# Turning the normalised rows with DMA transposes instead of TensorE transposes

## The chip, the cores and the metric

The kernel runs on one core of a Trainium2 chip. A core has TensorE (matrix products into PSUM), VectorE, ScalarE and GpSimd (element-wise work), and SyncE, whose queue issues the DMAs here; 16 DMA engines carry them. The metric is the device time of one execution in microseconds (us), lower is better.

## The reference

The input is x, 4096 rows (2 x 2048) of 1024 columns in fp32. For each row on its own:

```python
n = layernorm(x)
q, k, v = n @ wq.T + bq, n @ wk.T + bk, n @ wv.T + bv      # 1024 -> 1024, seen as 32 heads x 32
s = softmax(einsum("hd,td->ht", q, k) / sqrt(32))           # heads of one row attend to each other
x = x + einsum("ht,td->hd", s, v)
m = layernorm(x)
top2 gate of m @ gate_w.T (8 experts), softmax of the two
x = x + m @ base_w.T + base_b + 2 * sum over experts of gate * (m @ A_e.T) @ B_e.T   # rank 16
```

Attention goes over the 32 heads of one row, so no row needs another one.

## The kernel before, in words

It is written with explicit engine programs and semaphores. The rows are worked through in T = 32 tiles of 128 rows, one row a partition. Each engine has its own program of the same shape (`pipeline`): `step(0)`, a loop over t = 1 to 30 of `step(t, prev=True, nxt=True)`, `step(31, prev=True, nxt=False)`, and `tail(32)`. In step t the attention of tile t goes on beside the end of tile t-1 (attention's context, second layernorm, router and LoRA, base product, result) and the preparation of tile t+1 (first layernorm). The order of work on each engine is written out by hand, and an engine runs it strictly in that order.

All products are made with fp16 parts. A normalised row tile `xn` (fp32) is scaled and split into a high part (`x_hi` for the first layernorm, `x2_hi` for the second, an fp16 cast) and a low part (`x_lo`, `x2_lo`, what the cast left out). A product takes the parts in three combinations, or in two while the weights' low parts are zero, as they are for q, k and v here. TensorE needs the rows turned, with the 1024 columns on the partitions in 8 chunks of 128.

The steps that the change touches, by their order in a loop step t:

- TensorE: `project` runs k, q and v as two halves of 512 columns each. k half 1 and q half 0 have the context products of tile t-1 threaded between them (`attend_one`). After v half 0 comes `turn_rows(t-1)`: eight fp32 transposes of `xn` into PSUM (`turn_ps`). After v half 1 comes `experts(t-1)`: 24 products of 136 columns with router and LoRA weights, from `x2_hi` and `x2_lo`. Then `turn_rows(t+1)`, then `dense(0, k_parts)`: half of the base product, with the attention scores of tile t threaded in (semaphore `scored`), then `turn_low`, `dense(1)`, `dense_lora`.
- ScalarE: `rows_hi` casts each half of `turn_ps` to the high part. Tile t-1's comes after the high part of k, tile t+1's after the first quadrant copy of q (`spread_quadrant`), and behind that is the cast of the turned v (L568).
- VectorE: `normalise` writes `xn` (one buffer for both layernorms). `rows_lo` subtracts the high part from `turn_ps`, in two halves (L684). Tile t-1's comes after the first v bias, tile t+1's after `gating`; behind that VectorE waits for `scored` and takes the scores' maximum (L887).
- SyncE's queue: in each step the load of x tile t+1 into `ld`, the load of x tile t again as residual into `res`, and the store of tile t-1, each behind a wait for the buffer it uses.

At the start the weights of q, k, v, the small matrix `ag` (router and LoRA, rows of 544 bytes) and the base matrix are loaded, their maximum sums are taken on ScalarE (`sums`), and they are split into parts.

In the trace, tiles carved from one large buffer (`ld`, `xn`, `ev`, `turned`, `parts`, `k_parts`, `diag`, `soft`, `res`, `x1`, `y`) are all called work, and x2_hi and x2_lo appear as x_hi and x_lo.

Of the kernel before, what the change touches and what calls it, by code (L numbers as in the profile page):

```python
# [27 lines left out]
P = 128  # L28
# [34 lines left out]
def block_kernel(nc, x, wT, agT, lora_b, biases, out):  # L63
    T = x.shape[0] // P
    with ExitStack() as ctx:
# [117 lines left out]
        den = sb("den", [P, QD])  # L183
        inv = sb("inv", [P, QD])
# [15 lines left out]
        turn_ps = ps("turn_ps", [P, HID])  # L200
# [39 lines left out]
        xt_done = sem("xt_done")  # L240
# [38 lines left out]
        x2t_done = sem("x2t_done")  # L279
# [49 lines left out]
        def _(sp):  # L329
            sp.dma_start(ld, rows(x, 0)).then_inc(ld_loaded, 16)  # L330

            def load(g):
# [11 lines left out]
            load("k")  # L344
            load("q")
# [8 lines left out]

            sp.wait_ge(w_lo_done, n_split)
            sp.dma_start(res, rows(x, 0)).then_inc(res_loaded, 16)
# [17 lines left out]
            pipeline(sp, step, lambda t: store(t - 1))  # L374
# [86 lines left out]
        def _(act):  # L461
# [30 lines left out]
            def rows_hi(t, dst, done, ready):  # L492
                for h in range(2):

                    act.wait_ge(done, 2 * t + h + 1)
                    c = KC // 2
                    nc.scalar.copy(dst[:, h * c:(h + 1) * c, :],  # L497
                                   turn_ps[:, h * HALF:(h + 1) * HALF].rearrange("p (k n) -> p k n", k=c)
                                   ).then_inc(ready, 1)

            rows_hi(0, x_hi, xt_done, xhi_ready)
# [34 lines left out]
            def low_copy(p):  # L536
# [3 lines left out]
                nc.scalar.copy(low_t[:, :], low_ps[:, 0:P]).then_inc(lowt_ready, 1)  # L540

            def step(t, prev, nxt):
                if prev:
# [4 lines left out]
                    rows_hi(t - 1, x2_hi, x2t_done, x2hi_ready)  # L548
# [39 lines left out]
            def tail(t):  # L588
                rows_hi(t - 1, x2_hi, x2t_done, x2hi_ready)
# [7 lines left out]
        def _(dve):  # L597
# [81 lines left out]
            def rows_lo(t, dst, hi, hi_ready, ready):  # L679
                c = KC // 2  # L680
                for h in range(2):

                    dve.wait_ge(hi_ready, 2 * t + h + 1)
                    nc.vector.tensor_tensor(dst[:, h * c:(h + 1) * c, :],  # L684
                                            turn_ps[:, h * HALF:(h + 1) * HALF].rearrange("p (k n) -> p k n", k=c),
                                            hi[:, h * c:(h + 1) * c, :], ALU.subtract).then_inc(ready, 1)
# [46 lines left out]
            rows_lo(0, x_lo, x_hi, xhi_ready, xlo_ready)  # L733
# [70 lines left out]
            def norm2(p):  # L804

                dve.wait_ge(xt_done, 2 * p + 2)
# [21 lines left out]
            def step(t, prev, nxt):  # L828
# [9 lines left out]
                if prev:  # L838
                    norm2(t - 1)
# [4 lines left out]
                if prev:  # L844
# [3 lines left out]
                    rows_lo(t - 1, x2_lo, x2_hi, x2hi_ready, x2lo_ready)  # L848
                    if nxt:

                        dve.wait_ge(x2t_done, 2 * t)
# [74 lines left out]
            def tail(t):  # L926
                attention_end(t - 1)
                ln_stats(1, x1, mv2)
                norm2(t - 1)
                rows_lo(t - 1, x2_lo, x2_hi, x2hi_ready, x2lo_ready)  # L930
# [13 lines left out]

# [224 lines left out]
```

## Time and profile before

| | |
|---|---|
| median of 3 runs | 1545.02 us (1543.29 to 1545.65) |
| span of the profiled execution, first to last instruction | 1543.5 us |
| mean granted TensorE clock | 0.986 |
| TensorE products busy | 1367.9 us, 89% |
| VectorE busy | 1261.1 us, 82% |
| ScalarE busy | 503.8 us, 33% |
| GpSimd busy | 210.7 us, 14% |
| DMA moved | 70.52 MB, 46 GB/s over the span |

The profile was taken by the hardware on one execution. It has a span but no separate time of its own, so its 1543.5 us stand beside the runs: the median is 1.5 us above it. The time of a product is modelled and overlaps its neighbour's, so TensorE's 89% is not a share of its peak. "Idle before, released by" is the time that an engine stood before an instruction and what ended it. A granted clock of 1.00 is 2.4 GHz, 0.50 is 1.2 GHz.

### The profile page before, as it was taken

The page shows a single profiled execution, that of the slowest core. Times are in us where ns is not written, and L with a number is a line of the kernel's source. Part 1 is how long each engine was busy: PE and PEld are TensorE (multiplying, and loading weights), DVE is VectorE, ACT ScalarE, POOL GpSimd, SP SyncE. Part 2 cuts the span into 40 slices and gives each one's busy share as a digit, 9 for nine tenths or more (in the row PEclk, how much of TensorE's full clock was granted, in tenths as well). Part 3 has the DMA queues.
Part 4 walks back from the last instruction along what each step waited for, and adds up shares of the span by engine and source line. Part 5 has one row for each costly group of instructions (what it writes and reads, how often), then busy time and mean ns, then how long its engine had stood idle before and what let it go on. Part 6 is the DMA issues. An engine that isn't in the chain of part 4 may idle for free.

```text
span 1543.5 us, 30006 instructions
## 1 busy us (share of the span) xinstructions
PE 1367.9 (89%) x12432; PEld 750.4 (49%) x12432; DVE 1261.1 (82%) x1751; ACT 503.8 (33%) x572; POOL 210.7 (14%) x280
## 2 busy tenths in 40 slices
PE   0777999999999999999999999999999999999996
PEld 0444445545544554554455455445545544554553
DVE  5778888888888888888888888888888888888874
ACT  7952222333222233322223332222333222233320
POOL 0011110011111001111100111110011111001110
PEclk9989999999999999999999999999999999999997
DMA  9401111000111100011110101111000111100000
GB/s 380 165 1 42 41 41 37 31 29 25 41 41 41 37 31 29 25 41 41 41 35 33 31 23 41 41 41 36 32 31 24 41 41 41 38 30 30 24 29 28
DMA packets 20208, 70.52 MB, mean 46 GB/s; under 512 B 2144, under 2 KB 3168, under 8 KB 20192
## 3 DMA queue, kind: packets, MB, share of 16 engines
q1 hardware_dynamic: 20192, 70.30, 12.8%
q8 instruction: 11, 0.18, 0.1%
q14 instruction: 5, 0.04, 0.0%
HBM read 53.51 MB, written 16.78 MB: 46 GB/s over the span
## 4 chain that ended last, share of the span: by engine, by line
DVE 61%; PE 14%; issue 10%; ACT 6%; DVEq 5%; DMA 3%; SPq 0%; POOL 0%; ACTq 0%; POOLq 0%
DVE work L308 6%; DVE work L800 6%; DVE x_lo L684 5%; PE acc L965 5%; DVE work L725 5%; PE acc L976 5%; DVE work L872 4%; DVE work L843 4%; DVE work L718 4%; DMA work<-x_dram 3%; DVE work L794 3%; DVE work L889 3%; DVE work L911 3%; DVEq L751 3%; DVE work L906 2%
## 5 line engine op out<-in xcount | busy, mean ns | idle before, releaser
L1018 PE MATMUL acc<-base_parts,x_hi 128*128 128x512 f16 x1024 | 325.0, 381 | 32.4 <-DVE work L308 32.4
L956 PE MATMUL attn_ps<-work 128*128 128x32 f16 x2048 | 329.0, 177 | 2.7 <-DVE work L718 1.7
L957 PE MATMUL attn_ps<-work 128*128 128x32 f16 x2048 | 327.3, 176 | 0.0
L958 PE MATMUL attn_ps<-work 128*128 128x32 f16 x2048 | 326.9, 176 | 0.0
L957 PEld LDWEIGHTS attn_ps<-work 128*128 128x128 f16 x2048 | 189.7, 96 | 201.6
L308 ACT COPY work<-work 32x2048 f16<-32x2048 f16 x96 | 182.1, 1897 | 139.2 <-DVE work L718 88.3
L956 PEld LDWEIGHTS attn_ps<-work 128*128 128x128 f16 x2048 | 193.7, 96 | 6.0 <-issue 3.6
L965 PE MATMUL acc<-w_hi_k,x_hi 128*128 128x512 f16 x512 | 140.6, 385 | 62.1 <-DVE work L718 28.4
L1018 PE MATMUL acc<-base_parts,x_lo 128*128 128x512 f16 x512 | 194.4, 380 | 0.0
L958 PEld LDWEIGHTS attn_ps<-work 128*128 128x128 f16 x2048 | 188.9, 96 | 0.0
L668 DVE BATCH_NORM_STATS2 stats<-work 128x6 f32<-128x512 f32 x128 | 82.3, 685 | 126.4 <-DMA work<-x_dram 125.3
L718 DVE TENSOR_TENSOR work<-work 128x1024 f16<-128x1024 f32 x96 | 117.4, 1223 | 54.7 <-ACT work L568 37.9
L384 POOL TENSOR_TENSOR var<-mv,eps 128x1 f32<-128x1 f32 x64 | 12.1, 190 | 1072.2 <-DVE mv L671 1072.2
L497 ACT CAST x_hi<-turn_ps 128x512 f16<-128x512 f32 x128 | 68.1, 579 | 266.4 <-PE turn_ps L949 266.4
L725 DVE SCALAR_TENSOR_TENSOR work<-acc,acc_to_a,biases_sb 128x512 f32<-128x512 f32 x192 | 138.8, 736 | 12.3 <-PE acc L976 6.4
L1018 PEld LDWEIGHTS acc<-base_parts,x_hi 128*128 128x128 f16 x1024 | 101.2, 99 | 97.5 <-DVE work L308 39.4
L965 PE MATMUL acc<-w_hi_q,x_hi 128*128 128x512 f16 x512 | 138.5, 380 | 10.7 <-DVE work L725 8.4
L526 ACT CAST work<-work 128x1024 f16<-128x1024 f32 x32 | 33.4, 1045 | 336.9 <-DVE work L821 336.9
L976 PE MATMUL acc<-w_hi_k,x_lo 128*128 128x512 f16 x512 | 137.8, 379 | 0.0
L976 PE MATMUL acc<-w_hi_q,x_lo 128*128 128x512 f16 x512 | 137.2, 378 | 0.0
L965 PE MATMUL acc<-v_parts,x_hi 128*128 128x512 f16 x512 | 122.5, 383 | 8.0 <-DVE v_parts L640 8.0
L976 PE MATMUL acc<-v_parts,x_lo 128*128 128x512 f16 x512 | 121.0, 379 | 0.0
(135 smaller groups left out, 2231.4 us busy)
## 6 DMA issues: line engine op xcount, KB each, us to landing
work<-x_dram SPq DMA_DIRECT2D x64, 512.0 KB, 3.5
out_dram<-work SPq DMA_DIRECT2D x32, 512.0 KB, 2.8
work<-wT_dram SPq DMA_DIRECT2D x19, 512.0 KB, 9.5
v_parts<-wT_dram SPq DMA_DIRECT2D x8, 512.0 KB, 14.8
base_parts<-wT_dram SPq DMA_DIRECT2D x5, 512.0 KB, 12.1
biases_sb<-bias_dram SPq DMA_DIRECT2D x4, 512.0 KB, 15.2
work<-agT_dram SPq DMA_DIRECT2D x1, 544.0 KB, 4.7
lora_up<-lora_b_dram SPq DMA_DIRECT2D x1, 512.0 KB, 15.8
```

Source lines behind the costliest of these rows:

```text
L308: copy(diag[s, :, :, s], parts[s, :, :, :]).then_inc(ready, 1)
L668: nc.vector.bn_stats(stats[:, i, h, :], src[:, h * HALF:(h + 1) * HALF])
L684: nc.vector.tensor_tensor(dst[:, h * c:(h + 1) * c, :], turn_ps[:, h * HALF:(h + 1) * HALF].rearrange("p (k n) -> p k n", k=c), hi[:, h * ...
L718: nc.vector.tensor_tensor(parts[:, :, 1, :], turned3, parts[:, :, 0, :], ALU.subtract).then_inc(lo_ready, 1)
L725: nc.vector.scalar_tensor_tensor(out=ev[:, s], in0=acc[bank][:, :], scalar=acc_to_a[:, i:i + 1], in1=bias[g][:, s], op0=ALU.mult, op1=ALU. ...
L800: nc.vector.scalar_tensor_tensor(out=x1, in0=ev, scalar=ctx_undo[:, 0:1], in1=res, op0=ALU.mult, op1=ALU.add).then_inc(x1_ready, 1)
L956: nc.tensor.matmul(dst, diag[:, i, 0, :], moving[:, i, 0, :], start=True, stop=False)
L957: nc.tensor.matmul(dst, diag[:, i, 0, :], moving[:, i, 1, :], start=False, stop=False)
L958: return nc.tensor.matmul(dst, diag[:, i, 1, :], moving[:, i, 0, :], start=False, stop=True)
L965: nc.tensor.matmul(dst, x_hi[:, k, :], w_hi[g][:, k, cols], start=(k == 0), stop=False)
L976: mm = nc.tensor.matmul(dst, x_lo[:, k, :], w_hi[g][:, k, cols], start=False, stop=(k == KC - 1))
L1018: nc.tensor.matmul(dst, rows_part[:, m // 3, :], w_part[:, m // 3, cols], start=(m == 0), stop=False)
```

## The change

The normalised row tile is split before it is turned. ScalarE casts all of `xn` to `row_hi` (fp16), VectorE subtracts it from `xn` into `row_lo`, and SyncE's queue issues one DMA transpose for each part, from `row_hi` to `x_hi` or `x2_hi` and from `row_lo` to `x_lo` or `x2_lo`. TensorE's `turn_rows` and the PSUM tile `turn_ps` are gone. TensorE now waits for the transposes' landings (16 per transpose) before `experts` and before k half 0. ScalarE and VectorE wait, before they write `row_hi` or `row_lo` again, until the transpose that read it has landed. For tile t+1 the transposes are issued after v's last product of step t, since that reads the old `x_hi`. The first residual load moves behind the transposes of tile 1, and SyncE's loop is written out as 30 steps. Some small buffers share storage now.

```diff
+        row_hi = sb("row_hi", [P, HID], F16)
+        row_lo = sb("row_lo", [P, HID], F16)
         low = sb("low", [P, ER])
-        low_t = sb("low_t", [P, P])
-        den = sb("den", [P, QD])
-        inv = sb("inv", [P, QD])
+        den = top
+        inv = top
-        hot1 = sb("hot1", [P, EXPERTS])
-        hot2 = sb("hot2", [P, EXPERTS])
-        w_full = sb("w_full", [P, EXPERTS])
+        hot1 = best
+        hot2 = logits
+        w_full = best_no
-        turn_ps = ps("turn_ps", [P, HID])
...
+            def turn_rows(t, hi, hi_split, hi_ready, lo, lo_split, lo_ready):
+                sp.wait_ge(hi_split, t + 1)
+                sp.dma_start_transpose(hi[:, :, :], row_hi[:, :]).then_inc(hi_ready, 16)
+                sp.wait_ge(lo_split, t + 1)
+                sp.dma_start_transpose(lo[:, :, :], row_lo[:, :]).then_inc(lo_ready, 16)
+            def turn1(t):
+                turn_rows(t, x_hi, row1_hi, xhi_ready, x_lo, row1_lo, xlo_ready)
+            def turn2(p):
+                turn_rows(p, x2_hi, row2_hi, x2hi_ready, x2_lo, row2_lo, x2lo_ready)
...
             load("k")
+            turn1(0)
             load("q")
...
-            sp.wait_ge(w_lo_done, n_split)
-            sp.dma_start(res, rows(x, 0)).then_inc(res_loaded, 16)
...
                     sp.wait_ge(x1_ready, t)
                     sp.dma_start(res, rows(x, t)).then_inc(res_loaded, 16)
+                    turn2(t - 1)
+                if nxt:
+                    sp.wait_ge(v_acc, 2 * t + 2)
+                    turn1(t + 1)
+                if prev:
                     store(t - 1)
+                else:
+                    sp.wait_ge(w_lo_done, n_split)
+                    sp.dma_start(res, rows(x, 0)).then_inc(res_loaded, 16)
...
+            def rows_hi(t, xn_ready, turned_before, ready):
+                act.wait_ge(xn_ready, t + 1)
+                if turned_before is not None:
+                    sem_before, n_before = turned_before
+                    act.wait_ge(sem_before, n_before)
+                nc.scalar.copy(row_hi[:, :], xn).then_inc(ready, 1)
...
-                    rows_hi(t - 1, x2_hi, x2t_done, x2hi_ready)
+                    rows_hi(t - 1, xn2_ready, (xhi_ready, 16 * (t + 1)), row2_hi)
...
-                    act.wait_ge(v_acc, 2 * t + 2)
-                    rows_hi(t + 1, x_hi, xt_done, xhi_ready)
+                    rows_hi(t + 1, xn1_ready, (x2hi_ready, 16 * t) if prev else (xhi_ready, 16), row1_hi)
...
+            def rows_lo(t, split_hi, turned_before, ready):
+                dve.wait_ge(split_hi, t + 1)
+                if turned_before is not None:
+                    sem_before, n_before = turned_before
+                    dve.wait_ge(sem_before, n_before)
+                nc.vector.tensor_tensor(row_lo[:, :], xn, row_hi[:, :], ALU.subtract).then_inc(ready, 1)
...
-                    rows_lo(t - 1, x2_lo, x2_hi, x2hi_ready, x2lo_ready)
+                    rows_lo(t - 1, row2_hi, (xlo_ready, 16 * (t + 1)), row2_lo)
...
-                    dve.wait_ge(v_acc, 2 * t + 2)
-                    rows_lo(t + 1, x_lo, x_hi, xhi_ready, xlo_ready)
+                    rows_lo(t + 1, row1_hi, (x2lo_ready, 16 * t) if prev else (xlo_ready, 16), row1_lo)
...
             def experts(p):
-                pe.wait_ge(x2hi_ready, 2 * p + 2)
-                pe.wait_ge(x2lo_ready, 2 * p + 2)
+                pe.wait_ge(x2hi_ready, 16 * (p + 1))
+                pe.wait_ge(x2lo_ready, 16 * (p + 1))
...
-            turn_rows(0, xn1_ready, xt_done)
...
-                pe.wait_ge(xhi_ready, 2 * t + 2)
-                pe.wait_ge(xlo_ready, 2 * t + 2)
+                pe.wait_ge(xhi_ready, 16 * (t + 1))
+                pe.wait_ge(xlo_ready, 16 * (t + 1))
...
-                    turn_rows(t - 1, xn2_ready, x2t_done)
...
-                    turn_rows(t + 1, xn1_ready, xt_done)
```

## Rows read from the trace of the kernel before

**Rows 1.** The page: the chain that ended last, by engine.
```profile
DVE 61%; PE 14%; issue 10%; ACT 6%; DVEq 5%; DMA 3%; SPq 0%; POOL 0%; ACTq 0%; POOLq 0%
```

**Rows 2.** Timeline of TensorE, one step: start, length, instruction, count [idle before].
```profile
749.37 0.38 PE L965 MATMUL acc<-w_hi_k,x_hi 128*128 128x512 f16 x1 [0.95 <-DVE work L718]
...
763.87 1.89 PE L976 MATMUL acc<-v_parts,x_lo 128*128 128x512 f16 x8
766.84 1.09 PE L949 MATMUL turn_ps<-ident,work 128*128 128x128 f32 x8 [1.08 <-DVE work L676]
767.77 1.89 PE L965 MATMUL acc<-v_parts,x_hi 128*128 128x512 f16 x8
...
771.22 0.22 PE L1000 MATMUL acc<-ag_hi,x_hi 128*128 128x136 f16 x1
...
772.64 1.04 PE L949 MATMUL turn_ps<-ident,work 128*128 128x128 f32 x8
774.76 0.39 PE L1018 MATMUL acc<-base_parts,x_hi 128*128 128x512 f16 x1 [1.08 <-DVE work L308]
...
794.18 0.38 PE L965 MATMUL acc<-w_hi_k,x_hi 128*128 128x512 f16 x1 [0.95 <-DVE work L718]
```

**Rows 3.** Timeline of VectorE, the same step.
```profile
758.95 1.25 DVE L794 STREAM_TRANSPOSE work<-attn_ps 128x1024 f32<-128x1024 f32 x1 [0.29 <-PE attn_ps L958]
...
765.97 0.81 DVE L676 TENSOR_SCALAR work<-work,mv,rstd 128x1024 f32<-128x1024 f32 x1
...
769.41 1.28 DVE L684 TENSOR_TENSOR x_lo<-turn_ps,x_hi 128x512 f16<-128x512 f32 x2
...
782.41 1.28 DVE L684 TENSOR_TENSOR x_lo<-turn_ps,x_hi 128x512 f16<-128x512 f32 x2
783.61 1.21 DVE L887 TENSOR_REDUCE top<-attn_ps 128x32 f32<-128x1024 f32 x1
```

**Rows 4.** Groups by line, VectorE: count, busy us, mean ns, idle before.
```profile
L718 DVE TENSOR_TENSOR work<-work 128x1024 f16<-128x1024 f32 x96 | 117.4, 1223 | 54.7 <-ACT work L568 37.9
L725 DVE SCALAR_TENSOR_TENSOR work<-acc,acc_to_a,biases_sb 128x512 f32<-128x512 f32 x192 | 138.8, 736 | 12.3 <-PE acc L976 6.4
```

**Rows 5.** Timeline of ScalarE, the same step.
```profile
774.38 1.04 ACT L497 CAST x_hi<-turn_ps 128x512 f16<-128x512 f32 x2
...
782.61 1.90 ACT L308 COPY work<-work 32x2048 f16<-32x2048 f16 x1 [1.67 <-PE attn_ps L958]
```

**Rows 6.** DMA: the x loads, us to landing; window 3 to 7 us: packets, MB, share.
```profile
work<-x_dram SPq DMA_DIRECT2D x64, 512.0 KB, 3.5
...
q1 hardware_dynamic: 1283, 1.44, 104.4%
```

**Rows 7.** Windows (busy by engine, granted clock, DMA) and the TensorE work after two pauses.
```profile
74.50:75.00 0.50, 0.00 (x0) 0.00 (x0) 0.50 (x2) 0.50 (x1) 0.00 (x0) 0.87 0.88 311
78.50 3.46 PE L965 MATMUL acc<-v_parts,x_hi 128*128 128x512 f16 x8 [7.95 <-DVE v_parts L640]
81.50:82.00 0.50, 0.50 (x3) 0.21 (x2) 0.27 (x1) 0.19 (x1) 0.50 (x1) 0.80 0.00 0
122.50:123.00 0.50, 0.00 (x0) 0.00 (x0) 0.00 (x0) 0.00 (x0) 0.00 (x0) 0.66 0.97 393
126.72 3.25 PE L965 MATMUL acc<-w_hi_q,x_hi 128*128 128x512 f16 x8 [7.16 <-DVE work L725]
```

**Rows 8.** Timeline of the tail, VectorE's last normalisation and TensorE's experts.
```profile
1518.76 0.81 DVE L676 TENSOR_SCALAR work<-work,mv,rstd 128x1024 f32<-128x1024 f32 x1 [1.27 <-POOL rstd L389]
...
1523.09 0.27 PE L1000 MATMUL acc<-ag_hi,x_hi 128*128 128x136 f16 x1 [1.49 <-DVE x_lo L684]
...
1525.76 1.06 PE L1018 MATMUL acc<-base_parts,x_hi 128*128 128x512 f16 x2
```

**Rows 9.** Timeline of the start, VectorE's first normalisation and ScalarE's first sum.
```profile
7.10 0.81 DVE L676 TENSOR_SCALAR work<-work,mv,rstd 128x1024 f32<-128x1024 f32 x1 [1.28 <-POOL rstd L389]
10.52 0.32 ACT L477 ACTIVATE x_hi<-work 128x136 f16<-128x136 f32 x1
```

More of the change, by code:

```diff
@@ L239, in block_kernel @@
         xn1_ready = sem("xn1_ready")
-        xt_done = sem("xt_done")
+        row1_hi = sem("row1_hi")
+        row1_lo = sem("row1_lo")
         xhi_ready = sem("xhi_ready")
@@ L278, in block_kernel @@
         x1_biased = sem("x1_biased")
-        x2t_done = sem("x2t_done")
+        row2_hi = sem("row2_hi")
+        row2_lo = sem("row2_lo")
         x2hi_ready = sem("x2hi_ready")
@@ L371, in step, with tail @@
                     sp.dma_start(res, rows(x, t)).then_inc(res_loaded, 16)
-                    store(t - 1)
-            pipeline(sp, step, lambda t: store(t - 1))
+                    turn2(t - 1)
[3 more added lines that the diff above has]
+                if prev:
+                    store(t - 1)
+                else:
+                    sp.wait_ge(w_lo_done, n_split)
+                    sp.dma_start(res, rows(x, 0)).then_inc(res_loaded, 16)
+            def tail(t):
+                turn2(t - 1)
+                store(t - 1)
+            step(0, prev=False, nxt=True)
+            for t in range(1, T - 1):
+                step(t, prev=True, nxt=True)
+            step(T - 1, prev=True, nxt=False)
+            tail(T)
             sp.wait_ge(y_stored, 16 * (T + 1))
@@ L490, in high_parts @@
                                          scale=w_scale[:, j:j + 1]).then_inc(w_hi_act, 1)
[L492 to L501, printed above, removed]
+            def rows_hi(t, xn_ready, turned_before, ready):
[4 more added lines that the diff above has]
+                nc.scalar.copy(row_hi[:, :], xn).then_inc(ready, 1)
+            rows_hi(0, xn1_ready, None, row1_hi)
             sums("ag")
@@ L539, in low_copy @@
                 act.wait_ge(low_turned, p + 1)
-                nc.scalar.copy(low_t[:, :], low_ps[:, 0:P]).then_inc(lowt_ready, 1)
+                nc.scalar.copy(low[:, :], low_ps[:, 0:P]).then_inc(lowt_ready, 1)
             def step(t, prev, nxt):
@@ L588, in tail @@
             def tail(t):
-                rows_hi(t - 1, x2_hi, x2t_done, x2hi_ready)
+                rows_hi(t - 1, xn2_ready, (xhi_ready, 16 * t), row2_hi)
                 gate_exp(t - 1)
@@ L677, in normalise @@
                                         ALU.mult).then_inc(ready, 1)
[L679 to L686, printed above, removed]
+            def rows_lo(t, split_hi, turned_before, ready):
[4 more added lines that the diff above has]
+                nc.vector.tensor_tensor(row_lo[:, :], xn, row_hi[:, :], ALU.subtract).then_inc(ready, 1)
             a_steps = [0]
@@ L732, in _ @@
             normalise(0, 0, ld, rstd1, xn1_ready)
-            rows_lo(0, x_lo, x_hi, xhi_ready, xlo_ready)
+            rows_lo(0, row1_hi, None, row1_lo)
             scale("ag")
@@ L802, in attention_end, with norm2 @@
                 dve.wait_ge(x1_ready, p + 1)
-            def norm2(p):
-                dve.wait_ge(xt_done, 2 * p + 2)
+            def norm2(p, row_before):
+                dve.wait_ge(row1_lo, row_before)
                 normalise(p, 1, x1, rstd2, xn2_ready)
@@ L838, in step @@
                 if prev:
-                    norm2(t - 1)
+                    norm2(t - 1, t + 1)
                 dve.wait_ge(q_biased, 2 * t + 2)
@@ L847, in step @@
                     add_bias(t, 0, "v", 2, 1, v_acc, v_biased)
-                    rows_lo(t - 1, x2_lo, x2_hi, x2hi_ready, x2lo_ready)
+                    rows_lo(t - 1, row2_hi, (xlo_ready, 16 * (t + 1)), row2_lo)
                     if nxt:
-                        dve.wait_ge(x2t_done, 2 * t)
+                        dve.wait_ge(row2_lo, t)
                         normalise(t + 1, 0, ld, rstd1, xn1_ready)
@@ L928, in tail @@
                 ln_stats(1, x1, mv2)
-                norm2(t - 1)
-                rows_lo(t - 1, x2_lo, x2_hi, x2hi_ready, x2lo_ready)
+                norm2(t - 1, t)
+                rows_lo(t - 1, row2_hi, (xlo_ready, 16 * t), row2_lo)
                 gating(t - 1)
@@ L943, in _ @@
             pe.wait_ge(consts_set, EXPERTS + 4)
-            def turn_rows(t, xn_ready, done):
-                pe.wait_ge(xn_ready, t + 1)
-                for k in range(KC):
-                    mm = nc.tensor.transpose(turn_ps[:, k * P:(k + 1) * P], xn[:, k * P:(k + 1) * P], ident[:, :])
-                    if k % (KC // 2) == KC // 2 - 1:
-                        mm.then_inc(done, 1)
             def attend_one(moving, i):
@@ L1029, in dense_lora @@
                 for n in range(NB):
-                    nc.tensor.matmul(acc[1 + n][:, :], low_t[:, :], lora_up[:, n * HALF:(n + 1) * HALF],
+                    nc.tensor.matmul(acc[1 + n][:, :], low[:, :], lora_up[:, n * HALF:(n + 1) * HALF],
                                      start=False, stop=True).then_inc(base_acc, 1)
```

5 lines of the change are left out of this document (removed).

## The prediction

> **What bounds the kernel now.** I read the chain that ended last first: by engine it is 61% VectorE, 14% TensorE and only 3% DMA [rows 1]. Then I read one step of the loop on each engine, because nearly all of the span is 30 loop steps of one shape. Two neighbouring steps start the same TensorE instruction at 749.37 and 794.18, so a step takes 44.8 us [rows 2]. Inside it the chain changes hands once. From 749.37 TensorE runs the second half of k and the first half of q with the attention products of the tile before threaded between them, and VectorE gets the context at 758.95 [rows 2, 3]. From there to the next step's start VectorE sets the pace, and TensorE is ahead of it: it waits 1.08 us at 766.84 for the normalised row, 1.08 us at 774.76 for the spread queries and 0.95 us at 794.18 for the probabilities [rows 2]. So two things set the time: 9.6 us of TensorE at the head of the step, which the change doesn't touch, and 35.2 us of VectorE behind it. TensorE's transposes lie in the second part, where TensorE has time to spare.
>
> **Removed from TensorE.** Two groups of eight fp32 transposes a step. The first holds back the second half of v: the last eight products before it start at 763.87 and take 1.73 us, half of the 3.45 us of sixteen (767.77 to 771.22), so it could start at 765.6, and it starts at 767.77 [rows 2]. An earlier v is worth nothing while VectorE is the bound: its 192 bias additions, v's among them, waited for TensorE 6.4 us in the whole span [rows 4].
>
> **Changed on VectorE.** Two subtractions of 512 columns out of PSUM become one of 1024 columns out of SBUF. The pair takes 1.20 us from its start to the next instruction's (782.41 to 783.61) [rows 3]; one subtraction of the new shape takes 1.22 us [rows 4]. Between a gain of 0.1 and a loss of 0.1 us each I take zero. The small buffers that now share storage are used by VectorE in its own order, and the copy into low has the wait that it had: zero.
>
> **Changed on ScalarE.** Two casts of half a row (1.04 us together) become one of a row, which waits for the normalised row instead of for the transposes [rows 5]. It has a new wait too: the high transpose issued before it must have left the row buffer. For tile t+1 the cast can start at 774.38, where ScalarE casts today; queued behind it is the cast of the turned v, which VectorE waits for. The x2 high transpose lands at 773.2 by the price below, so this wait is over 1.2 us before; what it lands later than that cover goes on to VectorE.
>
> **Added: two DMA transposes for each normalised tile, two tiles a step, all on SP's queue.** No row shows one. Lower bound: an ordinary copy. The x load of 512 KB lands 3.5 us after its issue; a full queue moves 1.44 MB in 4 us, so 1.5 us of that is moving and 2.0 us is fixed, and 256 KB would take 2.8 us [rows 6]. For the middle I look for short runs: a row is turned in blocks of 128 columns, 1024 runs of 256 bytes. In the window that has the 544-byte rows of the small weight matrix, 1283 packets filled 104% of 16 engines for 4 us, 52 ns each [rows 6]. 64 runs an engine at 52 ns are 3.3 us, with the fixed part 5.3 us. I take that, because this row is nearest to it. Upper bound: each run costs twice, once read and once written turned: 6.6 us of moving, 8.6 us in all.
>
> Its place in the step. The normalised x2 row is done at 765.97 + 0.81 = 766.8 [rows 3] and the cast at 767.9; SP issues the high transpose then, and it lands at 773.2. VectorE's subtraction runs from 769.41 as now to 770.6, and SP issues the low one at 770.7. By itself it would land at 776.0, but its runs queue behind the high one's on the same engines and end 3.3 us after them: **776.5**. Today both parts are there when v ends at 771.22. Here lies the change's price: experts, the 24 products of router and LoRA, wait for that landing, and dense(0) with the attention scores is queued behind experts. It now starts at 774.76, and ScalarE is released by the scores at 782.61, so it takes 7.85 us [rows 2, 5]. VectorE takes the scores at 783.61 with no idle time [rows 3]: 1.0 us of slack.
>
> TensorE would stand still from 765.6 + 3.45 = 769.1 to 776.5, 7.4 us. What that does to its clock: idle since 70.55 (78.50 less 7.95), the granted clock drops near 74.9; idle since 119.56, near 122.7. That is 4.3 and 3.1 us after the last product. Work resumed at 78.50 has it back near 81.7, 3.2 us later [rows 7]. So experts run at 1.2 GHz: they take 2.7 us so in the tail (1523.09 to 1525.76) [rows 8], against 1.4 in the loop (771.22 to 772.64) [rows 2]. They end at 779.2, dense(0) loses 0.2 us until the clock is back at 779.7, and the scores are done at 779.2 + 8.05 = 787.2. VectorE, which wanted them at 783.6 with 0.1 for the release, stands 3.7 us; I take **3.6 us a step**. In general, with a landing at L, the stall is L - 772.9 at the low clock and L - 774.2 if the clock holds.
>
> The other landings are covered. Tile t+1's high part goes out near 775.5 and its low part at 783.7, after VectorE's second subtraction and ahead of the wait for the scores. It lands at 789.0; the half of k that needs it takes 3.45 us and ends 0.95 before 794.18 now, so it starts at 789.8 [rows 2], and with the stall at 793.4. The store and the x load queued behind it on SP wait for the end of the step in both kernels. The first residual load, now behind tile 1's transposes, still waits for the last weight split, which is later than they are.
>
> **Sum.** Steps 1 to 31 have experts of a tile before: 31 x 3.6 = 112 us (in the last one the scores come before the dense products, but those then end later by as much). Tail: the high part is issued at 1518.76 + 0.81 + 1.04 = 1520.6 and lands at 1525.9, the low one at 1529.2, where experts start at 1523.09 now [rows 8]: 6 us. Start: ScalarE's cast ends at 7.10 + 0.81 + 1.04 = 8.95 and the weights' sums begin there, instead of at 10.52 [rows 9]: -1.5 us, since the start hangs on those sums; q's loads are issued later behind tile 0's transposes, but ScalarE has the eight chunks of k before them. 112 + 6 - 1.5 is 116.5 on a span of 1543.5: 1660. The runs' median is 1.5 above this span, so **1661 us**.
>
> **Rivals.** (1) *A transpose is as quick as a copy and nothing happens.* At 2.8 us the low part lands at 773.5. If the clock holds through 4.4 us without work, there is no stall, and the tail's 1.6 us cancel the start's gain: 1545. It decides at a landing of 774.2, a transpose of 3.5 us. For it: no other transfer runs then. Against it: the short runs. The Trainium skill's Advanced Engine Details and Errata (X-Bar Transpose (TRN2)) states that such transposes are as fast as regular DMAs; no row here shows it, and by it the sum is this rival's. (2) *The same price, but the clock falls*, since 4.4 us is longer than both times above: 0.6 to 1.5 us a step, 1564 to 1592. (3) *Much slower transfers*, over 75 ns a run, or one transpose wholly behind the other. At the upper bound the high part lands at 776.5 and the low at 783.1: 10.2 us a step and 13 in the tail, 1872, and ScalarE's new wait then bites as well. For it: the writes turn the data. The skill's VectorE: DVE Perf Modes (The three transpose paths) gives 1309 ns for a 128x128 transpose by DMA against 390 on TensorE; eight such blocks are an estimated 10.5 us, and two in a row would land at 788.9, near 2050. That page speaks against the change. (4) *Faster.* The clock holds, the landing is before 774.2, and each of 62 subtractions saves the 0.1 us of its bound: 1539. It decides at 0.05 each.
>
> **How the numbers follow.** Chances: forecast (26 to 75 ns a run, landing at 774.4 to 779.5, 1592 to 1757) 0.48; rival 3 (above 1757) 0.22; rival 2 0.12; rival 1 0.13; rival 4 0.05. The time is the forecast's. The range leaves out rival 4 and the part of rival 3 beyond 85 ns a run: 1542 to 1800. No change can be told from a change within 0.2% here, 3.1 us. Faster 0.05, same 0.13, slower 0.82.
>
> **What the profile after would show.** Each transpose's time to landing (2.8, 5.3 or 8.6 us), and whether the low one lands a fixed time after the high; TensorE idle 7.4 us before experts, released by the DMA; a granted clock below 1.00 in every step; VectorE idle 3.6 us before the reduction of the scores, released by TensorE; subtractions of 1.2 us. It is wrong if a transpose lands in under 3.5 us, if VectorE stalls elsewhere (behind ScalarE's casts), or if issuing takes SP so long that the next tile's low part misses the k projection.

## The result and the profile after

| | before | after |
|---|---|---|
| median | 1545.34 us of 4 runs (1543.29 to 1546.83) | 1578.99 us of 4 runs (1578.48 to 1579.67) |
| span of the profiled execution | 1543.5 us | 1577.9 us |
| mean granted clock | 0.986 | 0.937 |

The ratio is 1.0217, with an interval of 1.0203 to 1.0232: slower, as forecast, but by 33.6 us and not by 116. The chain that ended last has turned over. Before it was 61% VectorE and 14% TensorE [rows 1]; here it is, by engine, on the page of the kernel after:

```profile
PE 61%; DVE 22%; DMA 7%; issue 6%; ACT 2%; DVEq 2%; POOL 0%; SPq 0%; POOLq 0%; ACTq 0%
```

**One step on TensorE**, the timeline that answers to [rows 2]:

```profile
735.34 1.89 PE L993 MATMUL acc<-v_parts,x_lo 128*128 128x512 f16 x8
741.95 0.27 PE L1017 MATMUL acc<-ag_hi,x_hi 128*128 128x136 f16 x1 [4.72 <-DMA x_lo<-row_lo]
...
744.62 0.63 PE L1035 MATMUL acc<-base_parts,x_hi 128*128 128x512 f16 x1
...
788.25 0.27 PE L1017 MATMUL acc<-ag_hi,x_hi 128*128 128x136 f16 x1 [4.46 <-DMA x_lo<-row_lo]
...
790.93 0.57 PE L1035 MATMUL acc<-base_parts,x_hi 128*128 128x512 f16 x1
```

v ends at 737.23, and experts start 4.72 us later, released by the low part's landing. They take 2.67 us (741.95 to 744.62) against 1.4 before, and the first dense product 0.63 us against 0.39 [rows 2].

**The transposes in the same step.** First SP's timeline, then the page's DMA issues (count, median us to landing), then the queue's row of the window 736 to 739 us (packets, MB, share of 16 engines):

```profile
736.10 1.24 SPq L337 DMA_TRANSPOSE x_hi<-row_hi  x1
738.78 1.23 SPq L339 DMA_TRANSPOSE x_lo<-row_lo  x1
743.68 1.23 SPq L337 DMA_TRANSPOSE x_hi<-row_hi  x1
751.88 1.23 SPq L339 DMA_TRANSPOSE x_lo<-row_lo  x1
```
```profile
x_hi<-row_hi SPq DMA_TRANSPOSE x64, 3.0
x_lo<-row_lo SPq DMA_TRANSPOSE x64, 3.0
```
```profile
q1 hardware_dynamic: 1056, 0.26, 45.5%
```

A transpose lands in 3.0 us. It is 1056 packets, and 45.5% of 16 engines for 3 us over 1056 is 21 ns a packet. The windows below (busy of PE, PEld, DVE, ACT, POOL; then granted clock, DMA share, GB/s) show both transposes and the clock:

```profile
737.00:737.50 0.50, 0.23 (x2) 0.00 (x0) 0.50 (x1) 0.50 (x1) 0.36 (x1) 1.00 0.36 73
737.50:738.00 0.50, 0.00 (x0) 0.00 (x0) 0.50 (x2) 0.42 (x1) 0.00 (x0) 1.00 1.08 213
738.00:738.50 0.50, 0.00 (x0) 0.00 (x0) 0.50 (x1) 0.00 (x0) 0.00 (x0) 1.00 1.12 207
738.50:739.00 0.50, 0.00 (x0) 0.00 (x0) 0.46 (x2) 0.00 (x0) 0.00 (x0) 1.00 0.17 31
739.00:739.50 0.50, 0.00 (x0) 0.00 (x0) 0.50 (x1) 0.00 (x0) 0.00 (x0) 1.00 0.00 0
739.50:740.00 0.50, 0.00 (x0) 0.00 (x0) 0.50 (x2) 0.00 (x0) 0.00 (x0) 1.00 0.04 8
740.00:740.50 0.50, 0.00 (x0) 0.00 (x0) 0.50 (x1) 0.00 (x0) 0.00 (x0) 0.61 1.03 209
...
746.50:747.00 0.50, 0.50 (x5) 0.23 (x4) 0.00 (x0) 0.47 (x1) 0.00 (x0) 0.56 0.00 0
```

Each part moves for about 1.3 us at some 210 GB/s, the high one from 737.3 to 738.6, the low one from 740.0 to 741.3, with idle engines between. So the low one never queues behind the high one. The granted clock falls to the 1.2 GHz level near 740.1, 2.9 us after v's last product, and is back near 746.95, 5.0 us after the work resumed. In the next step it falls at 787.9, 4.1 us after v's last product, and is back at 791.3, 3.1 us after the work resumed: 6.8 us at the low level in one step, 3.4 in the next.

**VectorE**, the timeline that answers to [rows 3], two steps, and then the sums of waits (us in total, times, longest) on the three engines:

```profile
706.81 1.23 DVE L912 TENSOR_REDUCE top<-attn_ps 128x32 f32<-128x1024 f32 x1 [0.67 <-PE attn_ps L975]
...
737.54 1.22 DVE L713 TENSOR_TENSOR row_lo<-work,row_hi 128x1024 f16<-128x1024 f32 x1
...
753.38 1.22 DVE L912 TENSOR_REDUCE top<-attn_ps 128x32 f32<-128x1024 f32 x1 [1.53 <-PE attn_ps L975]
```
```profile
PE acc L1017 <- DMA x_lo<-row_lo: 154.9, 32, 13.1
```
```profile
DVE top L912 <- PE attn_ps L975: 34.0, 30, 1.7
```

The wait for the scores, which did not exist before, is 34.0 us in 30 steps, alternately near 0.7 and 1.6; the long waits are those of the steps with 6.8 us at the low clock. That is the loss. I cut both spans at VectorE's first bias addition of step 1 and at the last normalisation, where the tail begins: start 120.41 and 119.32 us, loop 1398.35 and 1431.12, tail 24.74 and 27.46. The differences are -1.1, +32.8 and +2.7, in all +34.4 as the spans have it.

The loop's 32.8 is 34.0 of that wait, with smaller things beside it. Four more rows of the groups of VectorE moved (before to after): the wait for the x load 126.4 to 121.3 us, the residual add's own time 86.9 to 82.8, the wait for the context 8.0 to 12.3, and idle time before an 8-wide maximum of the gate 2.3 to 6.2. These are -5.1, -4.1, +4.3 and +3.9, with 34.0 together +33.0.

### The profile page after: what moved, and what is told of

It is laid out like the page before. It is cut to its first block, busy times and chain, and to the rows that moved or that the text cites. A ratio compares the mean times of both kernels' runs of the same rounds, so it can differ in the third digit from the quotient of the medians.

```text
span 1577.9 us, 28652 instructions
## 1 busy us (share of the span) xinstructions
PE 1353.9 (86%) x11920; PEld 734.5 (47%) x11920; DVE 1256.9 (80%) x1687; ACT 502.6 (32%) x508; POOL 210.5 (13%) x280
## 3 DMA queue, kind: packets, MB, share of 16 engines
q1 hardware_dynamic: 155360, 103.87, 23.8%
## 4 chain that ended last, share of the span: by engine, by line
PE 61%; DVE 22%; DMA 7%; issue 6%; ACT 2%; DVEq 2%; POOL 0%; SPq 0%; POOLq 0%; ACTq 0%
PE acc L1035 22%; PE acc L982 10%; PE acc L993 10%; DMA x_lo<-row_lo 6%; DVE work L827 5%; DVE work L870 4%; PE acc L1047 3%; PE attn_ps L975 3%; PE attn_ps L974 3%; DVE work L752 3%; DVE row_lo L713 3%; DVE work L821 3%; PE attn_ps L973 2%; PE acc L1017 2%; PE acc L1019 2%
## 5 line engine op out<-in xcount | busy, mean ns | idle before, releaser
L1035 PE MATMUL acc<-base_parts,x_hi 128*128 128x512 f16 x1024 | 337.8, 393 | 0.0
L974 PEld LDWEIGHTS attn_ps<-work 128*128 128x128 f16 x2048 | 193.3, 98 | 217.8 <-issue 23.6
L1017 PE MATMUL acc<-ag_hi,x_hi 128*128 128x136 f16 x256 | 79.4, 311 | 154.9 <-DMA x_lo<-row_lo 154.9
L973 PEld LDWEIGHTS attn_ps<-work 128*128 128x128 f16 x2048 | 196.0, 97 | 2.4 <-issue 2.2
L975 PEld LDWEIGHTS attn_ps<-work 128*128 128x128 f16 x2048 | 189.6, 96 | 0.0
L696 DVE BATCH_NORM_STATS2 stats<-work 128x6 f32<-128x512 f32 x128 | 82.3, 685 | 121.3 <-DMA work<-x_dram 120.1
L529 ACT CAST row_hi<-work 128x1024 f16<-128x1024 f32 x64 | 66.7, 1043 | 239.3 <-DVE work L704 239.3
## 6 DMA issues: line engine op xcount, KB each, us to landing
work<-wT_dram SPq DMA_DIRECT2D x19, 512.0 KB, 10.5
```

Of the source, the lines that this page charges most:

```text
L696: nc.vector.bn_stats(stats[:, i, h, :], src[:, h * HALF:(h + 1) * HALF])
L973: nc.tensor.matmul(dst, diag[:, i, 0, :], moving[:, i, 0, :], start=True, stop=False)
L974: nc.tensor.matmul(dst, diag[:, i, 0, :], moving[:, i, 1, :], start=False, stop=False)
L975: return nc.tensor.matmul(dst, diag[:, i, 1, :], moving[:, i, 0, :], start=False, stop=True)
L1017: nc.tensor.matmul(dst, x2_hi[:, k, :], ag_hi[:, k, :], start=(k == 0), stop=False)
L1035: nc.tensor.matmul(dst, rows_part[:, m // 3, :], w_part[:, m // 3, cols], start=(m == 0), stop=False)
```

## The experiments

The question was why this landing costs 1.1 us a step: in the prediction's times experts start at 773.8, and its rule for a clock that holds has no stall up to 774.2. Theory A: the clock. TensorE stands long enough for the granted clock to fall, experts and the next products run at half speed, and that takes more than the slack. Theory B: the landing alone comes too late, or the transfers themselves do the harm, whatever the clock. The kernels below start from the kernel after unless another is named; times are medians, and ratios are to the kernel before on the same chip (1545.1, 1546.94 and 1545.51 us in the three sets).

**1. Keep TensorE busy in the pause.** Products of weights into a spare PSUM tile, between v and experts; nothing reads them.

```diff
+                    keep_busy(16)
                     pe.wait_ge(q_biased, 2 * t + 2)
                     experts(t - 1)
```

> The changed kernel with 16 more products of 512 columns (2 times 1.73 us) on TensorE between v and experts, into an unused PSUM bank; their results are not used, and the landing of the low part stays where it is. Theory A, the clock: a landing 3.2 us after the issue fits under the slack as long as TensorE keeps 2.4 GHz; the loop's 33 us come from experts and the first dense products at 1.2 GHz. It expects a granted clock of 1.00 in the steps, VectorE idle 0 before the maximum of the scores, and 1546 to 1548 us (the start gives back 1.1 us, the tail keeps its 2.7). Theory B, the landing by itself: experts are queued behind it, and the clock only goes with that. It expects no change, 1579 us.

Measured: 1543.24 us, ratio 0.9988 (0.9978 to 0.9998). TensorE's timeline, and its windows over one step (same columns as above):

```profile
721.86 3.62 PE L1014 MATMUL spare_ps<-w_hi_k 128*128 128x512 f16 x16
726.83 0.22 PE L1023 MATMUL acc<-ag_hi,x_hi 128*128 128x136 f16 x1 [1.35 <-DMA x_lo<-row_lo]
...
728.25 0.38 PE L1041 MATMUL acc<-base_parts,x_hi 128*128 128x512 f16 x1
```
```profile
745.00:790.00 45.00, 43.26 (x384) 22.72 (x383) 37.75 (x51) 13.62 (x13) 6.37 (x8) 1.00 0.22 58
```

The transposes still land in 3.0 us and experts start 4.8 us after v's end (722.02), as late as before, but they take 1.42 us (726.83 to 728.25) at a clock of 1.00, and VectorE has no wait for the scores left. All of the 34 us went with useless work. A holds; B falls for the landing as it stands.

**2. Let the high part's products go first.** Experts' 16 products of x2_hi wait only for the high transpose, the 8 of x2_lo for both.

```diff
                 pe.wait_ge(x2hi_ready, 16 * (p + 1))
-                pe.wait_ge(x2lo_ready, 16 * (p + 1))
                 dst = acc[0][:, 0:AG]
                 for k in range(KC):
                     nc.tensor.matmul(dst, x2_hi[:, k, :], ag_hi[:, k, :], start=(k == 0), stop=False)
                     nc.tensor.matmul(dst, x2_hi[:, k, :], ag_lo[:, k, :], start=False, stop=False)
+                pe.wait_ge(x2lo_ready, 16 * (p + 1))
+                for k in range(KC):
```

> The changed kernel with experts in two groups: the 16 products with the high part wait for the high transpose alone, the 8 with the low part come behind them and wait for the low one. TensorE's pause of 4.6 us becomes two of under 2 us, and only 0.5 us of work is left behind the low landing. Theory A (clock) expects a clock of 1.00 in the steps, no VectorE idle time before the scores and 1545 to 1547 us. Theory B (landing) expects the work behind the landing to shrink by 0.9 us, so 0.9 us less stall a step, which leaves a mean of 0.2 and 1552 us, with the clock still falling.

Measured: 1552.97 us, 1.0049 (1.0033 to 1.0066). TensorE's timeline, and two windows:

```profile
728.08 0.23 PE L1016 MATMUL acc<-ag_hi,x_hi 128*128 128x136 f16 x1 [1.87 <-DMA x_hi<-row_hi]
...
730.74 0.88 PE L1020 MATMUL acc<-ag_hi,x_lo 128*128 128x136 f16 x8 [1.54 <-DMA x_lo<-row_lo]
```
```profile
730.00:730.50 0.50, 0.00 (x0) 0.00 (x0) 0.47 (x2) 0.50 (x1) 0.00 (x0) 1.00 0.27 51
732.00:732.50 0.50, 0.50 (x5) 0.23 (x4) 0.50 (x1) 0.49 (x1) 0.00 (x0) 0.50 0.00 0
```

The pause is cut in two, both under 2 us, and still the clock falls (1.00 at 730.0, 0.50 at 732.0). My expectation that it would not is wrong: light work between two pauses didn't hold the clock here. The time and the falling clock are those that theory B named (1552 us), so this run by itself doesn't decide for A. Beside run 1 it does: here the first dense product starts 5.6 us after v's end (726.21 to 731.82), there 6.2 us (722.02 to 728.25). Yet from it to ScalarE's release by the scores it takes 8.9 us here, at the low clock at first, and 7.8 there (to 740.75 and 736.09), and VectorE waits for the scores 7.5 us in all here, in 13 of the steps, and not at all there. Against the kernel after (7.4 us from v's end to the first dense product), the gain is that 16 of the 24 products are done before the low part lands, and before the fall at 731.0.

**3. Copies in place of transposes.** The rows reach x_hi and x_lo unturned.

```diff
-                sp.dma_start_transpose(hi[:, :, :], row_hi[:, :]).then_inc(hi_ready, 16)
+                sp.dma_start(hi[:, :, :], row_hi[:, :].rearrange("p (k n) -> p k n", k=KC)).then_inc(hi_ready, 16)
```

> The changed kernel with an ordinary DMA copy of the same bytes in place of each DMA transpose (the rows are not turned, so the products are of other numbers; all else is the same). It prices the turning. If a transpose is as quick as a copy: landing 3.0 us after the issue again, 1579 us. If the copy is quicker, by 2.0 us fixed and 0.7 us of moving: landing after 2.7 us, experts 0.5 us earlier (the transposes move for 1.3 us), the stall shrinks from 1.1 to about 0.6 us a step, 1564 us, or vanishes where the shorter pause keeps the clock.

Measured: 1552.97 us, 1.0050 (1.0033 to 1.0067). The page's DMA issues and the queue's whole row (packets, MB, share):

```profile
x_hi<-row_hi SPq DMA_DIRECT2D x64, 256.0 KB, 2.3
x_lo<-row_lo SPq DMA_DIRECT2D x64, 256.0 KB, 2.3
```
```profile
q1 hardware_dynamic: 38624, 103.86, 18.4%
```

A copy lands in 2.3 us, a transpose in 3.0. The queue's share over the whole span accounts for that: before it was 12.8% of 1543.5 us, here it is 18.4% of 1551.3 and in the kernel after 23.8% of 1577.9, so each of the 128 transfers keeps the 16 engines busy for 0.69 us as a copy (144 packets) and for 1.39 us as a transpose. The rest, 1.6 us, is the same for both. Even copies leave TensorE standing 3.75 us a step, and the clock falls (mean 0.945); the stall is only 7.6 us in all, in 7 of the 30 steps.

**4. The low part earlier.** VectorE's subtraction for x2 goes ahead of the first v bias.

```diff
-                    add_bias(t, 0, "v", 2, 1, v_acc, v_biased)
                     rows_lo(t - 1, row2_hi, (xlo_ready, 16 * (t + 1)), row2_lo)
+                    add_bias(t, 0, "v", 2, 1, v_acc, v_biased)
```

> The changed kernel with the x2 subtraction (row_lo) one place earlier on VectorE, ahead of the first v bias, so that the low transpose can be issued 0.7 us earlier. If only the issue time counts, the landing is 0.7 us earlier and TensorE's pause 3.9 us: the stall falls from 1.1 to about 0.3 us a step (the clock falls in part of the steps, as with the copy): 1552 us. Rival: the subtraction then runs from 736.9 while GpSimd is still at its bias addition (until 737.4), both out of SBUF; in the tail, where they overlap, this subtraction took 2.39 and not 1.22 us. Then it gains at most 0.2 us, the bias behind it is late, and the time stays within 5 us of 1579.

Measured: 1572.31 us, 1.0163 (1.0147 to 1.0179), between the two expectations. VectorE's timeline and its wait:

```profile
734.18 1.51 DVE L713 TENSOR_TENSOR row_lo<-work,row_hi 128x1024 f16<-128x1024 f32 x1
```
```profile
DVE top L912 <- PE attn_ps L975: 20.4, 26, 1.4
```

The subtraction starts 0.6 us sooner (2.83 us after the start of the normalisation of its tile in place of 3.43), but now lies beside GpSimd's bias addition, which ran from 732.24 to 734.61 in this step, and takes 1.51 us in place of 1.22. The low part is issued 2.4 us after the high one, in place of 2.7: TensorE stands 4.27 us a step in place of 4.57, and the stall shrinks by 13.6 us in all. The span shrinks by only 7.4 us (1577.9 to 1570.5): VectorE's row subtractions take 87.7 us in all in place of 78.9.

**5 and 6. The low part later, without and with work in the pause.** The x2 low transpose waits for a semaphore that comes about 2 us later; the second kernel also has 24 spare products.

```diff
                     sp.wait_ge(row2_lo, p + 1)
+                    sp.wait_ge(q_lo_ready, after)
                     sp.dma_start_transpose(x2_lo[:, :, :], row_lo[:, :]).then_inc(x2lo_ready, 16)
```

> The changed kernel with the x2 low transpose issued 2.0 us later in every loop step (SyncE waits for VectorE's low part of q before it). Together with the next run it parts landing and clock. Theory A: at 1.2 GHz there is no slack left, so each microsecond of the landing goes into the stall: 1579 + 30 x 2.0 = 1639 us, VectorE idle some 3.1 us a step before the scores. Theory B (landing alone) expects the same here, 1639.

> The same late low transpose, with 24 extra products of 512 columns (5.2 us) on TensorE in the pause of 6.6 us. Theory A: the clock stays at 2.4 GHz, so experts and the first dense products are 2.3 us shorter; of the 2.0 us of lateness the slack takes some 0.5 and 1.5 us a step stay: 1543 + 45 = 1588 us. So the landing has a price of its own once it is past the slack, and the clock adds some 50 us to it. Theory B expects no difference to the run before, 1639.

Measured: 1634.61 us, 1.0567 (1.0547 to 1.0586), without, and 1588.41 us, 1.0268 (1.0249 to 1.0287), with. VectorE's wait for the scores, first without and then with:

```profile
DVE top L919 <- PE attn_ps L982: 86.2, 30, 3.2
```
```profile
DVE top L920 <- PE attn_ps L983: 38.9, 30, 2.0
```

The mean granted clock is 0.921 without and 0.987 with. The same landing costs 2.87 us a step with TensorE idle and 1.30 with TensorE busy. So the landing by itself does cost once it is late enough; the clock adds 1.57 us on top. Put beside the prediction's two rules, whose stall is the landing less 772.9 at the low clock and less 774.2 at the high one, with a pause that begins at 769.1:

| kernel | TensorE waits for the low part, us a step | rule | stall by the rule | measured |
|---|---|---|---|---|
| copies | 3.75 | pause - 3.8 | 0 | 0.25 |
| early low part | 4.27 | pause - 3.8 | 0.5 | 0.68 |
| after | 4.57 | pause - 3.8 | 0.8 | 1.13 |
| late low part | 6.57 | pause - 3.8 | 2.8 | 2.87 |
| after, busy | (4.57) | pause - 5.1 | 0 | 0 |
| late low part, busy | (6.57) | pause - 5.1 | 1.5 | 1.30 |

The pauses are sums of waits without the tail's, over 31; those in brackets are those of the same landing without spare products; stalls are sums over 30. The rule of the low clock is 0.1 to 0.4 us too small, and in the right order; that of the high clock is 0.2 us too large in the one case where it gives a stall.

**7. The kernel before with SyncE's loop written out.** Nothing else of the change.

```diff
-            pipeline(sp, step, lambda t: store(t - 1))
+            step(0, prev=False, nxt=True)
+            for t in range(1, T - 1):
+                step(t, prev=True, nxt=True)
+            step(T - 1, prev=True, nxt=False)
+            store(T - 1)
```

> The kernel before with nothing changed but SyncE's loop, written out as 30 steps as the change does it. Part of the gain under the stall is not explained by the transposes: with the stall away the changed kernel is 2 us faster than before, and with DMA transposes for the first layernorm alone 5 us. The theory: the store and the next x load are issued 0.39 us apart instead of 0.89, the x load lands half a microsecond sooner, k and GpSimd's low part of k come sooner, and the residual addition overlaps less with GpSimd (its mean falls from 2717 to some 2580 ns, 4.4 us in all): 1541 us. Rival: the gain is the transposes' (no transposes of tile t+1 on TensorE, a subtraction out of SBUF), and this kernel stays at 1545.

Measured: 1540.89 us, 0.9958 (0.9944 to 0.9971). SP's timeline in the kernel before, then here:

```profile
750.07 0.36 SPq L361 DMA_DIRECT2D out_dram<-work  x1
750.96 0.33 SPq L367 DMA_DIRECT2D work<-x_dram  x1
```
```profile
748.43 0.34 SPq L361 DMA_DIRECT2D out_dram<-work  x1
748.82 0.43 SPq L367 DMA_DIRECT2D work<-x_dram  x1
```

The store is the last issue of one turn of the loop and the x load the first of the next. They stood 0.89 us apart and are now 0.39 apart. VectorE waits for that load in every step, and the median falls by 6 us, the loop in the trace by 3.6. The residual addition takes 83.5 us in all in place of 86.9, 3.4 us less, where the theory expected 4.4. This part of the change is a gain that had nothing to do with transposes.

**8 and 9. Only x1 by DMA.** The first layernorm's row is turned by DMA, the second's on TensorE as before (`pe_turn`, the eight fp32 transposes); the second kernel alone has the last two lines of the diff, 5 spare products behind experts.

```diff
-                    turn2(t - 1)
...
                project(t, "v", 0, 1, v_acc, any_low[0])
+                if prev:
+                    pe_turn(t - 1)
...
                     experts(t - 1)
+                    if nxt:
+                        keep_busy(5)
```

> One part of the change alone: the first layernorm's rows (x_hi, x_lo) are split and turned by DMA as in the changed kernel, the second layernorm's (x2_hi, x2_lo) are turned on TensorE and split out of PSUM as before. Both theories expect that this part costs nothing, because its landing is some 5 us ahead of the k projection: 1544 us, the start's 1.1 us under the kernel before. If instead something that both parts share costs time (the written-out loop of SyncE, 1.2 us of issue time a transpose, ScalarE's cast behind a new wait), a good part of the 33 us stays.

> The kernel with DMA transposes for the first layernorm alone, with 5 products of 512 columns (1.1 us) on TensorE behind experts, into a PSUM tile whose content is no longer needed. Without the transposes of tile t+1 there, TensorE stood 2.0 us before the dense products, the clock still fell in some steps (mean 0.976) and VectorE waited for the scores 3.2 us in all. Theory A expects a clock of 1.00 in the steps, that wait at 0, and 1537 us. If those 3 us are of another cause, 1540.

Measured: 1540.05 us, 0.9961 (0.9949 to 0.9974), and 1536.87 us, 0.9938 (0.9922 to 0.9953), with granted clocks of 0.976 and 0.986. The x1 transposes lie where nothing waits for them, so the first is level with the written-out loop alone (1540.89): the whole loss of the change is in x2's half. Spare products behind experts hold the clock through the wait for the spread queries, and the 3.2 us that VectorE waited for the scores in the first are gone in the second. The medians are 3.2 us apart, but they come from two sets, the spans of the two traces are 2.1 us apart and the intervals of the ratios overlap: the gain is near the noise.

**10 and 11. The x load before the store.** The rows of VectorE's groups said all along what the largest wait is: 126.4 us for the x load, which stands on SP behind a store that waits for the end of the step. Those rows, of the kernel before (count, busy us, mean ns, idle before), with the residual addition's:

```profile
L668 DVE BATCH_NORM_STATS2 stats<-work 128x6 f32<-128x512 f32 x128 | 82.3, 685 | 126.4 <-DMA work<-x_dram 125.3
L800 DVE SCALAR_TENSOR_TENSOR work<-work,ctx_undo 128x1024 f32<-128x1024 f32 x32 | 86.9, 2717 | 7.3 <-DVE work L794 7.3
```

In the tenth kernel (the one before, loop written out) the load of tile t+2 goes out as soon as `ld` is free; the eleventh has that and the edits of 8 and 9.

```diff
                     sp.dma_start(res, rows(x, t)).then_inc(res_loaded, 16)
+                if t + 2 < T:
+                    sp.wait_ge(xn1_ready, t + 2)
+                    sp.dma_start(ld, rows(x, t + 2)).then_inc(ld_loaded, 16)
+                if prev:
                     store(t - 1)
```

> The kernel before with SyncE's loop written out and the load of x tile t+2 issued in step t as soon as its buffer is free, ahead of the store's wait and not behind it. Theory: VectorE's 4 us wait for that load at the head of a step costs nothing by itself, since TensorE's 9.6 us of context products end at the same time; but it holds back VectorE's transpose of k, and with it ScalarE's and GpSimd's parts of k, and GpSimd's then overlaps VectorE's residual addition, 2.7 us in the loop against 1.28 us in the tail. Issued early, GpSimd is done before, the addition takes 1.3 us, and the time falls by some 1.3 us a step from the 1541 of the kernel with the written-out loop: 1500 us. Rival: the addition is slow for another reason, and all that is gained at the head is waited for at the context: 1541.

> Both together: DMA transposes for the first layernorm, the five products, and the early load. The gains should add, as they lie at different places: some 3 us under the run before, 1497 us; if the early load brings nothing, 1537.

Measured: 1497.54 us, 0.9688 (0.9675 to 0.9701), and **1492.59 us, 0.9652 (0.9639 to 0.9666)**, the fastest of all. Groups of VectorE in the tenth (count, busy us, mean ns, idle before):

```profile
L728 DVE SCALAR_TENSOR_TENSOR work<-acc,acc_to_a,biases_sb 128x512 f32<-128x512 f32 x192 | 139.2, 739 | 74.6 <-PE acc L979 68.7 <-ACT biases_sb L522 3.6 <-DVE lora_scale L652 0.2
L671 DVE BATCH_NORM_STATS2 stats<-work 128x6 f32<-128x512 f32 x128 | 82.0, 683 | 4.3 <-DMA work<-x_dram 3.1
...
L803 DVE SCALAR_TENSOR_TENSOR work<-work,ctx_undo 128x1024 f32<-128x1024 f32 x32 | 42.7, 1335 | 7.3 <-DVE work L797 7.3
L797 DVE STREAM_TRANSPOSE work<-attn_ps 128x1024 f32<-128x1024 f32 x32 | 40.0, 1250 | 63.9 <-PE attn_ps L961 63.9
```

The wait for x goes from 126.4 to 4.3 us. Nearly all of it turns into waits for TensorE: the bias additions 12.3 to 74.6 [rows 4], the context 8.0 to 63.9, 118 us of the 122. So the wait itself was worth some 4 us. The gain is the residual add, 86.9 to 42.7 us, since it no longer lies beside GpSimd's addition (below). The four changes make -122.1, +62.3, +55.9 and -44.2, together -48.1 us, on a span that is 49.5 shorter (of which the written-out loop alone has 4.0). The eleventh's remaining 5 us over the tenth are 1.8 at the start, 2.2 in the loop and -1.1 in the tail by the spans (2.9 in all); the medians of the two say 5.0.

## Why the prediction was wrong, and where it was right

**The step that failed** is the price of a transpose, 5.3 us: "64 runs an engine at 52 ns are 3.3 us, with the fixed part 5.3 us". Measured: 66 packets an engine at 21 ns are 1.4 us, with 1.6 fixed 3.0. The row it came from was misread. 1283 packets with 1.44 MB in 4 us [rows 6] have 1120 bytes on average, and another line of the same view says that only 44 of them are under 512 bytes:

```profile
DMA packets 1283, 1.44 MB, mean 359 GB/s; under 512 B 44, under 2 KB 1068, under 8 KB 1283
```

So the 52 ns are the time of a packet of 1120 bytes, and say nothing of what a short one costs. The runs have two more sizes: 21 ns for the transposes' packets of some 250 bytes (0.26 MB over 1056), and 77 ns for the copies' of 1820 bytes (0.69 us of 16 engines over 144). With the price fell the queueing ("its runs queue behind the high one's"): at 3.0 us the high part has landed when the low one starts to move. In the prediction's own times (this step lies 31.86 us earlier, 734.11 to 765.97) the low part was to land at 776.5; experts started at 773.8. A landing in under 3.5 us was also one of the prediction's own signs of being wrong. The lower bound was too high as well: 2.8 us with 2.0 fixed, and a copy took 2.3 with 1.6.

**What happened is rival 2**, given 0.12: a price near the copy's, but the clock falls, "0.6 to 1.5 us a step, 1564 to 1592". Measured 1.13 us a step and 1579. The forecast's own rule, with 773.8 in place of 776.5, gives 773.8 - 772.9 = 0.9 us a step.

**The other terms.** TensorE idle before experts: 7.4 forecast, 4.6 measured. Stall before the scores' maximum, released by TensorE: right in place and cause, 3.6 forecast, 1.1 measured. Tail: +6 forecast, +2.7 measured, where the cut at the last normalisation holds one thing more, a slow subtraction (below). Start: -1.5 forecast, -1.1 measured. VectorE's subtractions: one takes 1.22 us, as the row of the same shape said; zero was right. ScalarE's new wait: 2.2 us in the whole span before VectorE's subtraction, no cost. Tile t+1's parts: issued at 743.7 and 751.9, with SP free behind each; covered, as forecast, and the kernel with x1's half alone shows it. Clock: back after 3.2 us was read from [rows 7]; it was 5.0 us here and 3.1 in the next step, so the 0.2 us that dense(0) was to lose was too small. ScalarE's timeline has its release by the scores in the two steps:

```profile
753.43 1.90 ACT L310 COPY work<-work 32x2048 f16<-32x2048 f16 x1 [4.28 <-PE attn_ps L975]
...
798.96 1.90 ACT L310 COPY work<-work 32x2048 f16<-32x2048 f16 x1 [3.45 <-PE attn_ps L975]
```

From the first dense product (744.62 and 790.93) that is 8.8 and 8.0 us, against 7.85 before [rows 2, 5]: dense(0) loses 1.0 us in one step and 0.2 in the next, 0.6 in the mean. The 0.4 us over the forecast's 0.2 are what the rule misses for the kernel after (0.77 and 1.13).

**Missed.** The written-out SyncE loop was not costed; by itself it gives back 3.6 us of the loop. The 3.9 us before the gate's maximum were not seen either. That idle time (6.2 us) stands in the kernel after and in all six variants of runs 1 to 6, and not in the kernels of runs 7 to 11 (2.3 or 2.4 us), which turn x2 on TensorE. The eighth, ninth and eleventh share the small buffers too, so that is not the cause; it stays open.

**Rivals.** Rival 1 named a landing of 774.2 as its bound, and 773.8 is inside it: "if the clock holds" was the half that failed, and the busy kernel (1543.24) is rival 1 made true. The Trainium skill's Advanced Engine Details and Errata (X-Bar Transpose (TRN2)) has transposes as fast as regular DMAs; here it was 3.0 us against 2.3, a factor of two in the time that they move, and the measurement decides. That is far nearer than rival 3's estimate of 10.5 us from the Trainium skill's VectorE: DVE Perf Modes (The three transpose paths), which the trace doesn't bear out: eight blocks in one transfer take 3.0 us in all.

## What to carry to other kernels

A landing can be inside the slack and still cost: ask what the waiting engine's clock does in the pause, and what its next work costs at the lower level; here 16 useless products took back 36 us. A time per packet is read from a window whose packets are all of the size in question, since a full queue of larger ones shows only what those take. And before an engine off the critical path is relieved, look at the largest single wait of the one on it, and at what its end sets off beside the bound engine: here that was a load behind a blocked store. The wait itself was worth some 4 us, but the late load also pushed GpSimd's addition beside VectorE's, and moving it was worth 43 us (1540.89 to 1497.54), ten times the 4.0 us between the written-out loop (1540.89) and the best version with transposes by DMA and the old load (1536.87).

## What the runs showed of the hardware that was not expected

- TensorE's granted clock fell with two pauses of 1.87 and 1.54 us and light products between them, and not with 3.62 us of spare products and a pause of 1.35.
- The stall alternates between some 0.7 and some 1.6 us in neighbouring steps of the same work. In the step with 1.53 us the clock fell 2.9 us after v's last product and was back 5.0 us after the resumption; in the next, with 0.70, it fell after 4.1 us and was back after 3.1.
- Two SBUF operations of VectorE are slow beside GpSimd's. The residual add takes 2.65 us beside an operation of 2.12 us in the kernel before (both run from 760.44 to 762.00, 1.56 us), and 1.29 when GpSimd is idle (tenth kernel). The new subtraction takes 1.22 us in the loop and 2.39 in the tail, where GpSimd's bias addition runs from 1551.33 to 1553.67 (1.31 us of it beside the subtraction). So the excess is 1.36 us for 1.56 us side by side, and 1.17 for 1.31:

```profile
1550.44 0.81 DVE L704 TENSOR_SCALAR work<-work,mv,rstd 128x1024 f32<-128x1024 f32 x1 [1.27 <-POOL rstd L420]
...
1552.36 2.39 DVE L713 TENSOR_TENSOR row_lo<-work,row_hi 128x1024 f16<-128x1024 f32 x1 [1.11 <-ACT row_hi L529]
```

- Issuing a transpose holds SP for 1.23 us, against 0.47 for a copy of the same part and 0.33 to 0.43 for an x load.
- Leaving a loop's turn for the next costs SP about 0.5 us between two issues.
